# Six places for gathered rows, own one-hot tables for the last chunk, and a row list converted by the maximum

## The reference

```python
gate_scores = softmax(x @ Wg.T)                 # 8 experts
topk_val, topk_idx = top_k(gate_scores, 2)
comb = one_hot(topk_idx) * topk_val / (topk_val.sum() + EPS)
for e in range(8):
    h = x @ W1[e].T + b1[e]                     # 256 -> 1024
    a, b = split(h, 2)
    out += ((a * sigmoid(b)) @ Wo.T + bo) * comb[..., e]
```

## Time and profile before

| what | us |
|---|---|
| median of 3 runs | 600.7 |
| the profiled execution, its own time | 600.85 |
| its span | 599.0 |
| PE busy | 583.1 (97%) |
| DVE busy | 461.3 (77%) |
| ACT busy | 351.0 (59%) |
| POOL busy | 329.7 (55%) |

### The profile page before, as it was taken

One profiled execution on the slowest core, in us unless ns is written; L12 is line 12 of the kernel. 1 busy time (PEld: TensorE's weight loads), 2 busy tenths in 40 slices (PEclk: granted clock), 3 DMA queues, 4 the chain that ended last, 5 costly groups with the idle time before them and its releaser, 6 DMA issues.

```text
span 599.0 us, 21927 instructions
## 1 busy us (share of the span) xinstructions
PE 583.1 (97%) x8431; PEld 480.6 (80%) x8431; DVE 461.3 (77%) x1072; ACT 351.0 (59%) x768; POOL 329.7 (55%) x481
## 2 busy tenths in 40 slices
PE   8999999999999999999999999998899999999996
PEld 3888878888788888788888788886388878777695
DVE  4688867888678887677777687689778888887584
ACT  3677868878588888577777164545333333332462
POOL 3456867788668787678875222111346666664000
PEclk9999999999999999999999999999899999999999
DMA  8724553766544946693610399165424333344892
GB/s 230 182 68 119 149 188 94 242 162 213 153 148 147 264 118 219 167 247 125 210 41 4 125 435 400 65 204 198 156 95 132 133 131 134 130 131 126 314 343 75
DMA packets 65398, 102.13 MB, mean 170 GB/s; under 512 B 15280, under 2 KB 41968, under 8 KB 64400
## 3 DMA queue, kind: packets, MB, share of 16 engines
q1 hardware_dynamic: 59440, 84.59, 44.6%
q0 software_dynamic: 4992, 15.34, 7.7%
q10 hardware_dynamic: 864, 0.79, 0.5%
HBM read 69.43 MB, written 31.27 MB: 168 GB/s over the span
## 4 chain that ended last, share of the span: by engine, by line
PE 49%; POOL 20%; issue 15%; DVE 7%; DMA 4%; ACT 4%; DVEq 1%; POOLq 0%; SPq 0%; ACTq 0%
PE bank L1974 5%; PE bank L1048 5%; PE bank L1055 5%; PE bank L1080 4%; POOL hA L722 4%; POOL lA L718 4%; PE bank L2002 4%; POOL hA L714 4%; PE scores L1096 3%; PE scores L1069 3%; PE scores L1974 2%; DVE sg L1802 2%; DVE gg L1811 2%; PE scores L1232 2%; ACT sg L1916 2%
## 5 line engine op out<-in xcount | busy, mean ns | idle before, releaser
L854 DVE TENSOR_SCALAR Pm<-scores 128x514 f32<-128x514 f32 x128 | 88.1, 688 | 52.8 <-PE scores L1069 52.4
L970 ACT ACTIVATE Pm<-Pm,nm 128x257 f32<-128x257 f32 x256 | 115.8, 505 | 2.5 <-DVE nm L859 2.5
L859 DVE TENSOR_REDUCE nm<-Pm 128x2 f32<-128x514 f32 x128 | 87.5, 684 | 2.2
L965 ACT ACTIVATE PT<-bank 128x512 f32<-128x512 f32 x64 | 38.3, 598 | 74.3 <-PE bank L1080 74.3
L1048 PE MATMUL bank<-hA,wH 128*128 128x258 f32 x256 | 75.1, 304 | 0.3 <-POOL hA L722 0.3
L1080 PE MATMUL bank<-cst,Pm 128*128 128x128 f32 x512 | 70.0, 279 | 0.0
L1048 PE MATMUL bank<-hA,wL 128*128 128x258 f32 x256 | 69.2, 281 | 0.0
L1055 PE MATMUL bank<-wH,hA 128*128 128x256 f32 x256 | 68.9, 281 | 0.0
L1055 PE MATMUL bank<-wL,hA 128*128 128x256 f32 x256 | 68.8, 280 | 0.0
L1974 PE MATMUL bank<-W,xh 128*128 x208 | 66.8, 402 | 0.5 <-ACT xh L1904 0.5
L755 POOL TENSOR_TENSOR Mb<-Os,rc 128x64 f32<-128x64 f32 x64 | 21.8, 340 | 73.8 <-DVE rc L879 73.4
(11 more groups left out here) (289 smaller groups left out, 1453.6 us busy)
## 6 DMA issues: line engine op xcount, KB each, us to landing
w_d<-whl SPq DMA_DIRECT2D x64, 256.0 KB, 3.6
W<-w_d SPq DMA_DIRECT2D x6, 2048.0 KB, 17.5
wst<-in_W1T SPq DMA_DIRECT2D x32, 256.0 KB, 3.8
cg<-g_d SPq DMA_DIRECT2D x16, 512.0 KB, 6.2
cx<-in_ctxT SPq DMA_DIRECT2D x31, 258.0 KB, 3.0
cx<-in_ctxT SPq DMA_DIRECT2D x62, 129.0 KB, 3.5
bb<-in_b SPq DMA_DIRECT2D x8, 512.0 KB, 6.5
W<-w_d SPq DMA_DIRECT2D x5, 512.0 KB, 5.2
```

Of the source, the lines that this page charges most:

```text
L854: v.tensor_scalar(Pm[:, i % 2, 2 * p:2 * p + 2, :], S4[:, 2 * p:2 * p + 2, 0:NK], -CLAMP, CLAMP, ALU.max, ALU.min).then_inc(s_cl, 1)
L859: v.tensor_reduce(nm[:, i % 2, 2 * p:2 * p + 2], Pm[:, i % 2, 2 * p:2 * p + 2, :], AX.X, ALU.max, negate=True).then_inc(s_nm, 1)
L965: a.activation(PT[:, i % 2, 0, :, :].rearrange("p a b -> p (a b)"), held("p", i, 0)[:, :], ACT.Copy).then_inc(s_pte[0], 1)
L970: a.activation(Pm[:, i % 2, g, :], Pm[:, i % 2, g, :], ACT.Exp, bias=nm[:, i % 2, g:g + 1]).then_inc(s_ex, 1)
```

## The change

Four things are changed.

1. The last chunk has tables of its own, `A3` and `B3`. `marks(v, 3)` and `columns(a, 3, 1)` no longer wait for `slots` of chunk 2.
2. `Xg` has six places instead of four, and POOL gathers six tiles ahead. To make room, `gg2` moves to the area of `sg`, and `sg` has one place instead of two: the add of round i waits for the product of round i - 1.
3. The maximum writes the integer list `inv` from PSUM; the same maximum in floats is formed once more after it, since `ds` needs it.
4. Two semaphores are given up for the two new ones of `Xg`: the list `ds` is now told by `r_iv`, the bias added to `xb` by `u_ch`.

```diff
+        area(155, 161)
+        Xg = put("Xg", [128, 6, C])
         area(155, 159)
-        Xg = put("Xg", [128, 4, C])
+        A3 = put("A3", [128, 8, 128], F16)
+        B3 = put("B3", [128, 8, 128], F16)
...
+        def marked(c):
+            return (A3, B3) if c == 3 else (A16, Bv)
...
         def marks(v, c):
 
-            if c:
+            cols, vals = marked(c)
+            if 0 < c < 3:
                 v.wait_ge(u_iv, c)
...
-        sg = put("sg", [128, 2, 512])
-        gg = [put("gg0", [128, 512]), put("gg1", [128, 512])] + gg
+        sg = put("sg", [128, 512])
+        gg = [put(f"gg{i}", [128, 512]) for i in range(3)]
...
+                v.tensor_tensor(inv[:, :], bank("inv")[:, 0:40], neg[:, 0, :], ALU.max).then_inc(r_iv, 1)
                 link(v.tensor_tensor(neg[:, 1, :], bank("inv")[:, 0:40], neg[:, 0, :], ALU.max))
-                v.tensor_copy(inv[:, :], neg[:, 1, :]).then_inc(r_iv, 1)
...
                 columns(a, 2, 0)
-                a.wait_ge(u_iv, 3)
                 columns(a, 3, 1)
...
-                    if i >= 4:
-                        g.wait_ge(e_t, i - 3)
-                    g.indirect_dma_start(out=Xg[:, i % 4, :], out_offset=None, in_=y_d,
+                    if i >= 6:
+                        g.wait_ge(e_t, i - 5)
+                    g.indirect_dma_start(out=Xg[:, i % 6, :], out_offset=None, in_=y_d,
...
-                for i in range(4):
-                    gather(i)
-                g.wait_ge(r_ds, 1)
+                for i in range(6):
+                    gather(i)
+                g.wait_ge(r_iv, 2)
                 for i in range(NS):
-                    if i + 4 < NS:
-                        gather(i + 4)
+                    if i + 6 < NS:
+                        gather(i + 6)
...
-                if i >= 2:
-                    v.wait_ge(e_g, i - 1)
-                v.tensor_tensor(sg[:, i % 2, :], ab(i)[1][:, :], bf[:, bass.DynSlice(w + 512, 512)], ALU.add
+                if i:
+                    v.wait_ge(e_g, i)
+                v.tensor_tensor(sg[:, :], ab(i)[1][:, :], bf[:, bass.DynSlice(w + 512, 512)], ALU.add
```

More of the change, by code:

```diff
@@ L435, in slots @@
                 for j in range(4 * k, 4 * k + 4):
-                    mm = t.matmul(pI[:, 0:128], Bv[:, j, :], A16[:, j, :], start=(c == 0 and j == 0),
+                    mm = t.matmul(pI[:, 0:128], vals[:, j, :], cols[:, j, :], start=(c == 0 and j == 0),
                                   stop=(c == 3 and j == 7), skip_group_check=True)
@@ L492, in marks @@
                 mine = c < 2 or (c == 3) != (k == 1)
-                ins = v.tensor_tensor(Bv[:, 4 * k:4 * k + 4, :].rearrange("p j (e t) -> p j e t", t=16),
+                ins = v.tensor_tensor(vals[:, 4 * k:4 * k + 4, :].rearrange("p j (e t) -> p j e t", t=16),
                                       oht[:, c % 2, k, :, :].unsqueeze(3).broadcast_to([128, 4, E, 16]),
@@ L496, in marks @@
                 if mine:
-                    ins = v.tensor_tensor(A16[:, 4 * k:4 * k + 4, :], i16[:, :].unsqueeze(1).broadcast_to([128, 4, 128]),
+                    ins = v.tensor_tensor(cols[:, 4 * k:4 * k + 4, :], i16[:, :].unsqueeze(1).broadcast_to([128, 4, 128]),
                                           rests_of(c, k).unsqueeze(2).broadcast_to([128, 4, 128]), ALU.is_equal)
@@ L501, in columns @@
         def columns(a, c, k):
+            cols, _ = marked(c)
             for j in range(4 * k, 4 * k + 4):
-                a.activation(A16[:, j, :], i16[:, :], ACT.Abs, scale=-1.0, bias=rests_of(c, k)[:, j - 4 * k:j - 4 * k + 1]
+                a.activation(cols[:, j, :], i16[:, :], ACT.Abs, scale=-1.0, bias=rests_of(c, k)[:, j - 4 * k:j - 4 * k + 1]
                              ).then_inc(u_aa, 1)
             a.wait_ge(u_aa, 4 * (c - 1))
-            a.activation(A16[:, 4 * k:4 * k + 4, :], A16[:, 4 * k:4 * k + 4, :], ACT.Relu, scale=-1.0,
+            a.activation(cols[:, 4 * k:4 * k + 4, :], cols[:, 4 * k:4 * k + 4, :], ACT.Relu, scale=-1.0,
                          bias=cst[:, C_ONE:C_ONE + 1]).then_inc(u_as, 1)
-        area(159, 167)
+        area(161, 167)
         xh = put("xh", [128, 3, 2, 128], F32R)
         xl = put("xl", [128, 3, 2, 128], F32R)
-        gg = [put("gg2", [128, 512])]
         area(199, 207.75)
-        sg = put("sg", [128, 2, 512])
-        gg = [put("gg0", [128, 512]), put("gg1", [128, 512])] + gg
+        sg = put("sg", [128, 512])
+        gg = [put(f"gg{i}", [128, 512]) for i in range(3)]
         ds = put("ds", [128, 40], I32)
@@ L537, in build @@
         fo = put("fo", [128, NTILE, C])
-        r_ds = sem("r_ds")
-        r_b3 = sem("r_b3")
-        e_x = [sem(f"e_x{i}") for i in range(4)]
+        e_x = [sem(f"e_x{i}") for i in range(6)]
         e_t = sem("e_t")
@@ L1775, in gather @@
                 def gather(i):
-                    if i >= 4:
-                        g.wait_ge(e_t, i - 3)
-                    g.indirect_dma_start(out=Xg[:, i % 4, :], out_offset=None, in_=y_d,
+                    if i >= 6:
+                        g.wait_ge(e_t, i - 5)
+                    g.indirect_dma_start(out=Xg[:, i % 6, :], out_offset=None, in_=y_d,
                                          in_offset=bass.IndirectOffsetOnAxis(ap=inv[:, i:i + 1], axis=0)
-                                         ).then_inc(e_x[i % 4], 16)
-                for i in range(4):
+                                         ).then_inc(e_x[i % 6], 16)
+                for i in range(6):
                     gather(i)
-                g.wait_ge(r_ds, 1)
+                g.wait_ge(r_iv, 2)
                 for i in range(NS):
-                    if i + 4 < NS:
-                        gather(i + 4)
+                    if i + 6 < NS:
+                        gather(i + 6)
                     g.wait_ge(e_g, i + 1)
@@ L1810, in glu @@
                 v.wait_ge(e_sg, i + 1)
-                v.tensor_tensor(gg[i % 3][:, :], gg[i % 3][:, :], sg[:, i % 2, :], ALU.mult).then_inc(e_g, 1)
+                v.tensor_tensor(gg[i % 3][:, :], gg[i % 3][:, :], sg[:, :], ALU.mult).then_inc(e_g, 1)
             def final(v, j):
@@ L1851, in _ @@
                                             in1=neg[:, 1, :], op0=ALU.add, op1=ALU.mult))
-                v.tensor_tensor(ds[:, :], neg[:, 0, :], neg[:, 1, :], ALU.add).then_inc(r_ds, 1)
+                v.tensor_tensor(ds[:, :], neg[:, 0, :], neg[:, 1, :], ALU.add).then_inc(r_iv, 1)
                 v.wait_ge(r_sel, 3)
@@ L1873, in _ @@
                         v.scalar_tensor_tensor(out=xb[:, n, :], in0=bcc[:, 2, :], scalar=gs[:, 0, n:n + 1],
-                                               in1=xb[:, n, :], op0=ALU.mult, op1=ALU.add).then_inc(r_b3, 1)
-                v.wait_ge(r_b3, NTILE)
+                                               in1=xb[:, n, :], op0=ALU.mult, op1=ALU.add).then_inc(u_ch, 1)
+                        cnt[0] += 1
+                v.wait_ge(u_ch, cnt[0])
                 v.wait_ge(c_te, 1)
@@ L1915, in _ @@
                     a.wait_ge(e_ad, 2 * i + 1)
-                    a.activation(sg[:, i % 2, :], sg[:, i % 2, :], ACT.Sigmoid).then_inc(e_sg, 1)
+                    a.activation(sg[:, :], sg[:, :], ACT.Sigmoid).then_inc(e_sg, 1)
                 a.wait_ge(e_h, 2 * NS)
@@ L1951, in turn @@
                 def turn(i):
-                    t.wait_ge(e_x[i % 4], 16 * (i // 4 + 1))
+                    t.wait_ge(e_x[i % 6], 16 * (i // 6 + 1))
                     if i >= 2:
@@ L1955, in turn @@
                     for k in range(2):
-                        mm = t.transpose(tb(i)[:, 128 * k:128 * k + 128], Xg[:, i % 4, 128 * k:128 * k + 128], ident)
+                        mm = t.transpose(tb(i)[:, 128 * k:128 * k + 128], Xg[:, i % 6, 128 * k:128 * k + 128], ident)
                     mm.then_inc(e_t, 1)
```

## The result

The changed kernel takes 598.66 us (median of 14 runs), the kernel before, timed beside it, 601.82 (14 runs). The two medians lie 3.2 us apart; the ratio estimated from all the runs is 0.9959, with a 95% interval of 0.9946 to 0.9973, which is 2.5 us less, between 1.6 and 3.2. It stood on record as 598.5, and faster by 2.33 us.

What follows compares the result with a forecast made beforehand. The loop was taken as bound by PE, so only its waits or slowdowns could be won: 0.60 (tables) + 0.23 (row list) + 1.5 (six places) = 2.33 us off 600.85, giving 598.5, range 597.5 to 600.5.

Steps and rivals of the forecast that it cites:

- The loop, six places: Expert loop: gathers get 9.5 us of lead against at most 4.1 of landing; 1.5 us saved, bounds 1.16 and 1.61.
- The Trainium skill's figure: Gathers in the loop: 2.3 us for 128 KB, so all land in time, six places give nothing, total 600.0.
- The tables: End of the routing: chunk 3's own tables remove PE's 0.43 wait before the second four matmuls; 0.60 us saved, bounds 0 and 0.95.
- slots(3) begins behind it at 425.03 in any case: End of the routing: PE's filler at the lower clock runs to 425.0, so slots(3) starts no earlier despite earlier tables.
- The upper bound of 0.95: End of the routing: the tables' most possible gain, DVE's own, if PE were free.
- the second half follows the first: slots(3) on PE: the second four matmuls start at 425.25 instead of 425.85, without waiting for ACT's table; 0.60 us earlier.
- The signs named in the prediction: Profile after: among others, first gather near 427.5, L1974's first matmul near 432.7, turns 2.97 to 3.00 apart.
- The row list: Routing's end: one linked step fewer up to inv, 0.23 us saved; the second gather's wait, 0.68, falls to 0.45 and still decides.
- One place of `sg`: DVE adds in the loop: the added wait costs 0, bounds 0 and 0.26 us.
- rivals, 1 and 4: 1: head only, no loop gain, 600.0, chance 0.12. 4: new places do nothing, 600.7, chance 0.03.
- Rival 2: Routing's end: loop only, the tables' gain given back at the lower clock, 599.1 us; chance 0.15.
- Rival 3: Start of the loop: the clock falls if the second gather lands late, slower at 603.3 us; chance 0.05.

Runs made afterwards that it cites:

- The two comparisons of whole times: Changed kernel (598.82 us) against itself with four places of Xg (600.29); six places without new tables (599.54) against one place of sg with four (601.30).
- the repeat: The changed kernel timed once more, unedited, against the kernel before: 598.82 us, ratio 0.9969.
- the leanest kernel: Changed kernel with late second transposes, two fillers instead of three after the row list, none ahead of the product with sel: 598.10 us, ratio 0.9947.

## Why the prediction was right

**The loop, six places.** The mechanism, more lead for the gathers, is shown: three, four, five and six places give 4.38, 3.02, 2.975 and 2.974 a step, the first near the 4.1 of the ring that was worked out (which counts POOL's order, not free places), and late turns vanish from five on. The size, 1.5, agrees with 1.55 in the two profiles, but it was taken from one execution with many late turns, so a part of the agreement is luck. The five profiles with four places take 107.77 to 108.70 for their 36 steps (mean 108.2), the five of the loop as changed, with five or six, 107.04 to 107.71 (mean 107.2): 1.0 us is the mean gain, give or take 0.5. The two comparisons of whole times say 1.5, as forecast, with 0.5 to 2.5 and 0.9 to 2.2. So 1.0 to 1.5 is the best reading, and whether the term was too large by as much as a third of itself stays open. The Trainium skill's figure, DMA: Bandwidth & Descriptors (Anatomy of one DMA), 2.3 us by an estimate from it, isn't borne out here: landings are 2.8 at the median and up to 4.1 after the change too, and the places gain what it would have denied. In two other profiles with five and six places one landing took 4.9 and 4.6, and no turn was late.

**The tables.** 0.60 was forecast, 0.7 to 0.9 came. The step that was mis-sized is "slots(3) begins behind it at 425.03 in any case": it took the clock's return at 424.8 as given. It is not; where the clock returns earlier PE's filler is shorter, PE waits for DVE (0.20 in the profile after), and the gain is bounded by the tables. The upper bound of 0.95 for that case held, and so did "the second half follows the first" in the profiles with a late clock. There the forecast is nearly met: with the clock back 6.0 after the product the head is 0.71 shorter than before at 6.2. The signs named in the prediction came 0.7 to 0.8 early (first gather 426.76 for 427.5, first matmul 432.00 for 432.7): 0.27 of it arose ahead of the rank product, the rest in the head.

**The row list.** 0.23 forecast, 0.24 and 0.23 found, and the wait for the second gather did go on deciding (0.49 left of 0.68, forecast 0.45).

**What was put at nothing.** One place of `sg`: 0.9998. The seven gathers ahead of the first store delay nothing: the seventh is issued at 434.55, the first store at 437.95, and the first matmul comes 5.74 after `inv`, as before (5.68). The tail is 55.34 in both; that it agrees so closely is chance, for in the other profiles it is 55.45 to 56.22, over code that is the same.

**The sum.** With the measured sizes it is 0.7 to 0.9 + 0.23 + 1.0 to 1.5 = 1.9 to 2.6, against 2.33 forecast and 2.5 (1.6 to 3.2) timed, 1.9 in the repeat (ratio 0.9969). The forecast lies inside, with the tables put a little too low and the places perhaps too high. Each part alone was under or near what timing can tell (0.9975, 0.9989, 0.9999): the tables' gain is read from profiles, and no timing shows it. Of the rivals, 1 and 4 are refuted by the six places alone (0.9959 to 0.9992) and by three places. Rival 2 has the right object, the clock, and the wrong effect as far as the profiles reach: a later return makes the head longer with either tables, and with the clock back 5.5 to 6.2 after the product the tables still gain. At about 8 there is no profile with one pair, so whether their gain would be lost there isn't shown. Rival 3 did not happen: the clock is 1.00 throughout the loop.

## What to carry to other kernels

A gather that is issued behind another step of the loop runs in a ring: add up one trip, from the turn whose product lets the store and then the gather go, to the turn that uses the gather (here 8.2 us for two rounds with three places), divide by the rounds it spans, and compare with the round of the bound engine. Where the quotient is only a little under the round (2.75 against 2.97), late landings and slow steps still come through; here one more place took them all, and a second one added nothing. Look also at how long a place had stood free when its gather was issued (here 9.6 us): if long, the order of the issues, and not the room, sets the lead. And before a gain in a short stretch is read from two profiles, look at the granted clock in both: here 0.4 of 1.10 us was the clock's.

## What was not expected of the hardware

- At the end of the routing PE's gap of 1.9 us is followed by a fall of the granted clock, in the gap or up to 1.1 us behind it, in all thirteen profiles that have it. The stretch at 0.50 is either 3.4 us long (five profiles) or 6.8 (eight), and nothing between, for code ahead of it that is the same. It is 3.4 where the fall came between 0.1 us ahead of the rank product and 0.8 behind it, and 6.8 where it came earlier (0.6 to 1.3 ahead) or later (1.1 behind). The same head takes 7.7 to 9.1 us by that.
- Filling the gap of 1.91 us made a gap of 1.88 elsewhere, and the clock fell there instead.
- Steps of an unhindered loop are 2.97 in most profiles and 2.99 to 3.00 nearly throughout in two (the six places alone, and the leanest kernel), with the DVE add 1.66 after the turn in both kinds. What makes the difference of 0.7 us over the loop wasn't tried and stays open.
- An execution's time varies by some 4 us, of which up to 2.4 stand already at 418 us, ahead of all that was changed.
